# Graph kernel of four layers: the last layer's dense rows and final scatters go straight into the output

## What is computed

```
h = relu(layernorm(x))
h_src = h[src];  z_src = h_src @ Ws.T;  z_dst = h[dst] @ Ws.T;  z_e = he @ Ws.T
e   = concat([z_src, z_e, z_dst], 1) @ Wa.T
msg = einsum('ei,eio->eo', h_src, W_rel[rel_type]) * e
x   = x + segment_sum(msg, dst, num_segments=100000)
```

## Time and profile before

| | |
|---|---|
| median of three runs | 6354.33 us (6350.84 to 6355.94) |
| profiled execution, span | 6351.4 us |
| last layer within it | 5320.4 to 6351.4 us |
| busy: POOL, DVE, PE, ACT | 4351.5, 3600.2, 2978.8, 1200.2 us |
| DMA queues over the span: q1 (SP), q0 (POOL) | 13.8%, 8.2% of 16 engines |

### The profile page before, as it was taken

The page is one execution under the profiler, slowest core; times in us unless marked ns, Lnnn a source line. Parts: engine busy times, 40 slices in busy tenths (PEclk is TensorE's granted clock), DMA queues, the critical chain, the costliest instruction groups (busy, mean ns, idle before and its releaser), DMA issues. The chain is left out here.

```text
span 6351.4 us, 45625 instructions
## 1 busy us (share of the span) xinstructions
PE 2978.8 (47%) x13326; PEld 2237.0 (35%) x13326; DVE 3600.2 (57%) x8950; ACT 1200.2 (19%) x1944; POOL 4351.5 (69%) x3949
## 2 busy tenths in 40 slices
PE   5789599993544454436654553111111126553000
PEld 2477555552433343335543443111111113442000
DVE  8855389996556567764356778433322128886000
ACT  0256355541322233312111110000000001000000
POOL 4766555556776377747767776888888843777776
PEclk9899799995666555557667775555555567876555
DMA  2022122221111322213332222222222235221001
GB/s 43 15 67 64 53 69 66 67 66 37 20 20 18 79 63 69 63 39 105 99 98 63 69 69 76 54 37 37 37 34 25 12 74 188 60 56 36 7 7 46
DMA packets 283359, 350.16 MB, mean 55 GB/s; under 512 B 133519, under 2 KB 204433, under 8 KB 281971
## 3 DMA queue, kind: packets, MB, share of 16 engines
q1 hardware_dynamic: 112158, 295.24, 13.8%
q0 software_dynamic: 169376, 41.40, 8.2%
q10 hardware_dynamic: 1576, 10.60, 0.7%
HBM read 231.06 MB, written 122.29 MB: 56 GB/s over the span
## 5 line engine op out<-in xcount | busy, mean ns | idle before, releaser
L2362 POOL DMA_INDIRECT acc<-l_rows,l_uniq x392 | 623.0, 1589 | 120.0 <-issue 108.8
L526 POOL DMA_INDIRECT pay<-in_x,gidx x392 | 466.3, 1190 | 241.2 <-DMA pay<-in_x,gidx 108.3
L2403 PE MATMUL ps_l<-l_msg,l_alike 128*128 128x16 f32 x784 | 176.1, 375 | 961.1 <-DVE l_msg L2466 961.1
L814 POOL DMA_INDIRECT t_sort<-pay,c_pos x392 | 385.9, 984 | 295.2 <-DVE c_pos L880 194.9
L1497 POOL DMA_INDIRECT g_ring<-t_gat,idx x392 | 422.4, 1077 | 230.2 <-issue 112.6
L2632 POOL DMA_INDIRECT l_ring<-t_last,idx x392 | 387.6, 989 | 266.7 <-ACTq L2626 146.7
L1827 POOL DMA_INDIRECT r_ring<-t_rel,idx x392 | 427.8, 1091 | 186.2 <-issue 108.5
L906 PE MATMUL ps_c<-plane,c_hit 128*128 128x400 f32 x1568 | 542.5, 499 | 0.7 <-ACT c_hit L832 0.7
L2348 POOL DMA_INDIRECT l_ring<-t_mix,idx x392 | 426.2, 1087 | 154.8 <-issue 119.1
L2403 PEld LDWEIGHTS ps_l<-l_msg,l_alike 128*128 128x128 f32 x784 | 170.8, 330 | 966.4 <-DVE l_msg L2466 966.4
L2138 POOL DMA_INDIRECT r_ring<-t_rel,idx x392 | 394.6, 1007 | 152.9 <-issue 110.4
(11 more groups left out here) (530 smaller groups left out, 8202.7 us busy)
## 6 DMA issues: line engine op xcount, KB each, us to landing
c_rows_d<-row_dst SPq DMA_DIRECT2D x98, 256.0 KB, 3.3
l_keys<-row_at SPq DMA_DIRECT2D x49, 512.0 KB, 4.0
l_typs<-row_typ SPq DMA_DIRECT2D x49, 512.0 KB, 3.7
g_hs<-t_gat SPq DMA_DIRECT2D x30, 660.0 KB, 4.7
acc<-r_zero SPq DMA_DIRECT2D x60, 320.0 KB
t_rel<-r_row SPq DMA_DIRECT2D x30, 640.0 KB, 3.5
r_hs<-t_rel SPq DMA_DIRECT2D x30, 640.0 KB, 4.7
d_gain<-acc SPq DMA_DIRECT2D x30, 640.0 KB, 6.1
```

Source lines behind the costliest of these rows:

```text
L526: pool.indirect_dma_start(pay[:, s, 8:PAY], None, x, bass.IndirectOffsetOnAxis(gidx[:, s:s + 1], 0)).then_inc(gat_in[s // BATCH], 16)
L814: pool.indirect_dma_start(t_sort, bass.IndirectOffsetOnAxis(pos[:, e:e + 1], 0), pay[:, e, :], None).then_inc(sent, 16)
L2362: pool.indirect_dma_start(acc[r], bass.IndirectOffsetOnAxis(uniq[:, s:s + 1], 0), rows[:, (s // ES) % RR, s % ES, :], None, compute_op=ALU.add
```

## The change

The tensor `fin` is gone. The dense write goes to `out` and takes only the 125 partitions that hold nodes. The scatters go to `out` as well and carry a bound of 99,999; a row whose index lies above it is not written and not reported as an error. The copy at the end and its wait are gone. All lines after L115 move up by one.

```diff
-    fin = scratch("fin", (NP + P * (T + 1), FEAT))
...
-            dense_out, copied = sem("dense_out"), sem("copied")
+            dense_out = sem("dense_out")
...
                         spaced(pool, sent, s)
-                        pool.indirect_dma_start(fin, bass.IndirectOffsetOnAxis(home_i[:, s:s + 1], 0),
-                                                X[:, s, :], None).then_inc(sent[s // BATCH], 16)
+                        pool.indirect_dma_start(out, bass.IndirectOffsetOnAxis(home_i[:, s:s + 1], 0), X[:, s, :], None,
+                                                bounds_check=N - 1, oob_is_err=False).then_inc(sent[s // BATCH], 16)
                     all_landed(pool, sent, 0, T + 1)
                     all_landed(pool, gat_in, 0, T)
...
                 def _(sp):
-                    sp.dma_start(fin[0:NP].rearrange("(p c) f -> p c f", c=C), XD[:]).then_inc(dense_out, 16)
+                    sp.dma_start(out.rearrange("(p c) f -> p c f", c=C), XD[0:NPART]).then_inc(dense_out, 16)
...
                     all_landed(sp, sent, 0, T + 1)
-                    sp.dma_start(out.rearrange("(p c) f -> p (c f)", c=C),
-                                 fin[0:N].rearrange("(p c) f -> p (c f)", c=C)).then_inc(copied, 16)
-                    sp.wait_ge(copied, 16)
```

## The result

| | before | after |
|---|---|---|
| median, 11 runs each | 6348.45 us (6337.11 to 6355.94) | 6363.89 us (6357.46 to 6369.56) |
| ratio, 95% interval | | 1.0026 (1.0017 to 1.0035) |
| span of the profiled execution | 6351.4 us | 6360.1 us |
| from the layer's first gather to the end | 1030.3 us | 1045.3 us |

What follows compares the result with a forecast made beforehand. POOL's issuing of gathers and scatters was taken to bound the layer, so its delays are paid in full. -9.8 + 20 + 5.5 = +15.7 us on 6354.3 gave 6370.0 us; range 6343 to 6415, the forecast's own 6360 to 6380.

Steps and rivals of the forecast that it cites:

- Term 1: End of kernel: removing the copy saves 9.8 us, not 23.4, because the closing barrier then waits for POOL's drain.
- Term 2: Gathers: the 125-partition dense write runs on 5 engines and stalls POOL before gathers 16 and 24, +20 us.
- Term 3: Scatters: the bound costs 0 to +0.63 us on each, taken as 0.014, +5.5 us in all.
- (a): Rival, scatters: the bound is dear, every 0.1 us being 39 us, up to 6612 us; chance 0.21.
- (b): Rival, scatters: skipped rows make them cheaper, 0.21 us each, 82 us in all, giving 6282 us; chance 0.11.
- (c): Rival, gathers: the dense write stalls nobody, on 16 engines or in small packets; 6344.5 us, 6350 with the bound; chance 0.13.
- (d): Rival: only part of the stall, a store running faster on the five engines, or the drain shrinking; 6350 to 6362; chance 0.11.

Runs made afterwards that it cites:

- x4: The kernel before with its last copy cut to 128 rows, leaving the output unfilled: ratio 0.9987 to before, tail 16.2 us against 26.0.
- x2: The kernel before with its dense write on 125 partitions, still to fin: ratio 1.0025 to before, gathers 528.8 us against 507.9.
- x3: The changed kernel with its dense write cut into ten column pieces of 5,120 B packets: ratio 0.9997 to before, gathers 513.2 us.
- x7: The changed kernel with the bound's register loaded once instead of before every scatter: ratio 1.0029 to before, scatters still 973 ns.
- x5: The kernel before with a bound on each scatter that no index exceeds: ratio 1.0004 to before, scatter mean 973 ns.
- x6: The kernel before with bound 99,999 on each scatter, still into fin, skipping 10,986 rows: ratio 1.0009 to before, scatter mean 973 ns.
- x8: The changed kernel with POOL waiting at the end for only the last three scatter batches: ratio 1.0018 to before, tail 12.1 us.

## Why the prediction was right

The forecast was +15.7 us against the profiled execution. It measured +15.0 from the first gather on, and the ratio's interval of 11 to 22 us holds the forecast. The ratio, 1.0026, lies on the slower side of the line that the prediction drew at 0.2%, but its interval reaches down to 1.0017, so that this side is likely and not certain. The absolute figure, 6370.0, came out 6 us above the median, because it stood on the three runs that gave 6354.3 for before, and eleven gave 6348.45.

- **Term 1, -9.8: measured -9.5.** The drain's mechanism is shown by x4. After the change the waits were 5.8 us where I took 5.5, and the drain 9.38 where it had been 9.28.
- **Term 2, +20: measured +19.0 in the changed kernel, 20.9 in x2.** Gather 16 came 16.0 us later, as worked out, and gather 24 19.3. Five engines (29.8%), one q0 packet for each dense one (5 and 5 in the 2 us at 5342), and a dense packet of about 2 us were all seen; from its first packet to its last the write took 49.1 us, forecast 49.5. x2 shows the cause, x3 that it is the packet's length. I put the stalls at 16 and some 5 us; they were 17.15, in which the 1.15 of before is contained, and 4.17. The difference between 19.0 and 20.9 is within the noise of the gathers. DVE's first selector was 52 us into the layer (5366.2 - 5314.2), forecast 55.6, and was covered as I had argued: POOL's waits name DVE nowhere. That this cover is thin is shown by x3: without POOL's stall, DVE's lateness is what POOL meets next.
- **Term 3, +5.5: measured +5.4.** The size was right by luck, not by reasoning. I took the difference between two forms of DMA, which has nothing to do with a comparison. The two parts that I had costed at nothing, the register loads and the skipped rows, are shown to be nothing by x7 and by x5 beside x6.
- **The rivals.** (a) and (b) fell: a bound is neither dear nor does skipping save anything. (c) fell for this change, but its mechanism is real: with packets of 5,120 B on the same engines the stall is gone. A packet of the length that the Trainium skill ("DMA: Bandwidth & Descriptors", "SWDGE vs HWDGE vs iDMA") prefers, 4096 B, was not what this transfer had. x3, with 5,120 B, is the nearest run, and there the longest wait for a gather was 0.3 us; no run here has 4096 B. (d) fell by its mechanism, though the median, 6363.89, is only 2 us above its range: the stall was there whole, a store ran on five engines like the loads, and the drain did not shrink.

## What to carry to other kernels

A copy that ends the program is worth only what it sticks out past the other engines' ends; look for POOL's drain under it before you count its whole length. When a transfer is narrowed to leave out unused partitions, work out on how many engines it will run and how long one packet is, and then ask which small DMAs share these engines: here 2% fewer bytes cost 20 us through gathers that nobody had touched. A long transfer that nothing waits for did least harm here when cut into short pieces and placed behind the loads that are needed first; the cutting brought most of it.

## What the runs showed of the hardware

- **A skipped row is not left out.** These rows are those of POOL's queue over the whole span, first in x5, which has a bound above all rows, and then in x6, which skips 10,986 and is otherwise the same:

```profile
q0 software_dynamic: 169376, 41.40, 8.1%
```

```profile
q0 software_dynamic: 169376, 40.74, 8.2%
```

The count of packets is the same and 0.66 MB are missing, which is 60 B for each skipped row of 64 B. So 4 B seem still to move for each; what they carry and where they go is not shown. That fits a scatter whose time does not depend on how many rows are skipped.

- **POOL's drain after the last scatters took 9.28 us** whether it began 1.4 us (x8) or 5.5 us (before, x4) after the last one, and 9.38 at 5.8 us. What it waits for is not shown.
- **The number of partitions set the number of engines.** A write of 128 partitions ran on 16 engines at 2.0 us for a packet of 51 KB, one of 125 partitions on 5 engines at 1.9 (29.8% of 16 engines for 2 us, over 5 packets). One of 112 partitions, with 13 more in a DMA behind it, kept 16 engines busy, with packets of 2.0 us in one stretch and 2.5 us in another.
